# Layer 0's attention: the bias of two heads added as alternating 64-row tiles instead of one 128-row tile at a time

## What is computed

```python
B, N, C = x.shape                                   # 2, 1024, 128
H, D = (HEADS, C // HEADS)                          # 16 heads of 8
energy = jnp.einsum('bhqd,bhkd->bhqk', q, k)
pos = jnp.arange(N)
rel = pos[:, None] - pos[None, :] + (N - 1)
rel = jnp.clip(rel, 0, bias_table.shape[0] - 1)     # 0 .. 248
bias = bias_table[rel].transpose(2, 0, 1)
energy = energy + bias[None]
att = jax.nn.softmax(energy / (scaling * temp), axis=-1)
out = jnp.einsum('bhqk,bhkd->bhqd', att, v)
```

## Time and profile before

| | |
|---|---|
| timed executions | 1321.68, 1335.06, 1337.76 us |
| profiled execution, its own time | 1324.57 us |
| its span | 1322.7 us |
| TensorE busy | 1142.0 us, 86% |
| VectorE busy | 806.7 us, 61% |
| ScalarE busy | 650.9 us, 49% |
| layer 0's attention | about 228 to 663 us of the span |
| mean granted TensorE clock | 0.889 |

### The profile page before, as it was taken

How to read it: one execution, slowest core, us unless ns; L and a number is a source line. 1 busy time by engine, 2 the same in 40 slices (tenths; PEclk the granted TensorE clock), 3 DMA queues, 4 the chain that set the end, 5 groups by cost and what they waited for, 6 DMA issues and landing times.

```text
span 1322.7 us, 18522 instructions
## 1 busy us (share of the span) xinstructions
PE 1142.0 (86%) x6826; PEld 531.8 (40%) x6826; DVE 806.7 (61%) x1582; ACT 650.9 (49%) x1247; POOL 193.5 (15%) x309
## 2 busy tenths in 40 slices
PE   6599999999899999998884875899998889878577
PEld 4366666222222322232142432444443657434344
DVE  6633333878699889885056854787882524536554
ACT  4332222167477778777524143666777222414344
POOL 2146553001010011101000000112231000001000
PEclk9699999579799999999586586889999889899789
DMA  4521224133101101100006331110132300000321
GB/s 131 183 86 54 79 87 103 32 75 77 39 19 34 42 22 31 35 10 18 9 9 207 83 74 38 49 49 20 60 115 87 109 0 0 1 1 0 128 105 55
DMA packets 62165, 77.93 MB, mean 59 GB/s; under 512 B 15760, under 2 KB 39936, under 8 KB 60032
## 3 DMA queue, kind: packets, MB, share of 16 engines
q1 hardware_dynamic: 62080, 76.81, 19.1%
HBM read 61.58 MB, written 14.56 MB: 58 GB/s over the span
## 4 chain that ended last, share of the span: by engine, by line
PE 68%; DVE 13%; DMA 6%; SPq 5%; ACT 5%; issue 2%; POOL 0%; DVEq 0%; ACTq 0%
PE PS L1482 66%; DVE mx L1276 4%; ACT arena L877 3%; SPq L526 3%; DMA sums<-arena 2%; DMA arena<-k_dram 1%; SPq L533 1%; DVE arena L1455 1%; DVE small L1439 1%; SPq L544 1%; PE PS L1495 1%; DMA arena<-drev_dram 1%; DVE arena L1090 1%; DVE arena L1093 0%; DMA arena<-mrow 0%
## 5 line engine op out<-in xcount | busy, mean ns | idle before, releaser
L1482 PE MATMUL PS<-arena 128*32 128x512 f32 (+13 forms) x3656 | 626.9, 495 | 68.5 <-DVE mx L1276 39.3
L877 ACT ACTIVATE arena<-PS 128x512 f32<-128x512 f32 (+3 forms) x896 | 438.7, 556 | 271.3 <-PE PS L1482 267.5
L1276 DVE TENSOR_REDUCE mx<-PS 128x1 f32<-128x512 f32 (+3 forms) x896 | 506.5, 624 | 102.7 <-PE PS L1482 98.9
L1482 PEld LDWEIGHTS PS<-arena 128*32 128x32 f32 (+3 forms) x3656 | 160.2, 105 | 446.3 <-DVE mx L1276 181.2
L1482 PE MATMUL PS<-x_hi,w_hi_lo 128*128 128x512 f32 x320 | 145.1, 495 | 0.8 <-DVE combT L1154 0.4
L1377 DVE TENSOR_TENSOR fw<-PS,fw 128x512 f32<-128x512 f32 x80 | 55.3, 691 | 119.8 <-ACT fw L924 118.0
L924 ACT ACTIVATE fw<-PS 128x512 f32<-128x512 f32 x80 | 47.8, 597 | 123.5 <-PE PS L1482 123.5
L815 POOL TENSOR_TENSOR fw<-fw,arena 128x512 f32<-128x512 f32 x64 | 84.9, 1327 | 88.9 <-DVE fw L1377 88.9
L1482 PE MATMUL PS<-arena,fw 128*128 128x512 f32 x128 | 72.4, 680 | 24.7 <-DVE arena L1455 20.8
L1482 PE MATMUL PS<-fw 128*128 128x512 f32 (+3 forms) x184 | 90.6, 579 | 0.0
L768 POOL TENSOR_TENSOR arena<-arena,fw 128x512 f32<-128x512 f32 x32 | 41.7, 1304 | 268.7 <-DMA fw<-sum_dram 268.7
(11 more groups left out here) (268 smaller groups left out, 1035.4 us busy)
## 6 DMA issues: line engine op xcount, KB each, us to landing
arena<-comb_dram SPq DMA_DIRECT2D x16, 1024.0 KB, 5.1
fw<-sum_dram SPq DMA_DIRECT2D x32, 256.0 KB
arena<-comb_dram SPq DMA_DIRECT2D x16, 512.0 KB, 7.4
arena<-k_dram SPq DMA_DIRECT2D x16, 408.0 KB
q_dram<-arena SPq DMA_DIRECT2D x24, 256.0 KB, 3.8
k_dram<-arena SPq DMA_DIRECT2D x24, 256.0 KB, 3.9
arena<-q_dram SPq DMA_DIRECT2D x16, 384.0 KB
arena<-drev_dram SPq DMA_DIRECT2D x32, 192.0 KB, 3.7
```

Of the source, the lines that this page charges most:

```text
L877: s.activation(Pr[:, m % 8, 0:w], bank(4 + m % 3, 0, w), ACT.Exp).then_inc(A["e_done"], 1)
L1276: v.reduce_max(mx[:, H % 2, kh, n:n + 1], bank(U % RING, 0, w), axis=AX.X, negate=True).then_inc(A["ring_free"], 1)
L1482: return nc.tensor.matmul(out_, lhsT, rhs, start=start, stop=stop)
```

## The change

Per head and part, the bias now lies as two 64-row tiles in the row half in which that head's Q and K lie. `flip_sw` is `flip` with its row halves exchanged. Each former 128-row matmul becomes two 64-row ones, one for each half of the mirror. In ST these have 128 weight columns and 64 moving columns, half as many as before; in S five of six have 64 weight columns (half of the output's partitions) and the last one has 128, with 256 or 128 moving columns as before. The two heads of a pair (j even and j odd) are issued together: product, product, then the additions of both in turn. The tests `first_of_pair` and `second_of_pair` keep a pair in one slot of the plan. Layer 1 keeps its order.

```diff
@@ s_plan
+    if layer == 0:
+        marks = [n + first_of_pair(stream[n - 1]) for n in marks]
...
-            while i < len(steps) - 1 and done * t_total >= total * t_done:
+            while i < len(steps) - 1 and done * t_total >= total * t_done and not (layer == 0 and second_of_pair(what)):
@@ buffers
-        drev_dram = dram("drev_dram", (GROUPS, HG, PARTS, DREV), BF16)
+        drev_dram = dram("drev_dram", (GROUPS, HG, 2, PARTS, DREV), BF16)
+        flip_sw = sb("flip_sw", [P, P], BF16)
-        Hst = bf(132, 12).rearrange("p (s j a c) -> p s j a c", s=2, j=HG, a=PARTS)
+        Hst = bf(132, 12).rearrange("p (s r x c) -> p s r x c", s=2, r=PAIRS, x=2 * PARTS)
@@ load_bias
-                    src = bass.AP(tensor=drev_dram.tensor, offset=G * (HG * PARTS * DREV) + j * PARTS * DREV,
-                                  ap=[[1, P], [DREV, PARTS], [1, 256]])
-                    sp.dma_start(Hst[:, parity, j, :, :], src).then_inc(h_ld[parity], 16)
+                    row = 64 * (j % 2)
+                    src = bass.AP(tensor=drev_dram.tensor, offset=(G * HG + j) * 2 * PARTS * DREV,
+                                  ap=[[1, 64], [DREV, 2 * PARTS], [1, 256]])
+                    sp.dma_start(Hst[row:row + 64, parity, j // 2, :, :], src).then_inc(h_ld[parity], 16)
@@ stores of drev_dram, and the waits for them (16 * PARTS * BATCH * 2)
-                    dst = drev_dram[b * NG:(b + 1) * NG, :, part, :].rearrange("g j n -> (g j) n")
-                    sp.dma_start(dst, dpart[:, part, :]).then_inc(drev_stored, 16)
+                    for half in range(2):
+                        dst = drev_dram[b * NG:(b + 1) * NG, :, half, part, 0:DREV - 64 * half].rearrange("g j n -> (g j) n")
+                        sp.dma_start(dst, dpart[:, part, 64 * half:DREV]).then_inc(drev_stored, 16)
@@ GpSimd's constants: a memset of flip_sw and two affine_selects on it, ahead of const_done
+                    (flip_sw, [[1, P]], -(P // 2 - 1), 1, ALU.not_equal, 1.0),
+                    (flip_sw[:, :], [[1, P]], -(P + P // 2 - 1), 1, ALU.not_equal, 1.0),
@@ TensorE: additions to an S unit
-                        for part in range(PARTS):
-                            ins = mm(bank(U % RING, h0, 512), flip[:, :], Hst[:, G % 2, j, part, 0:512 - h0], start=False, stop=part == PARTS - 1)
+                        for part in range(PARTS):
+                            for half in range(2):
+                                rows = slice(64 - 64 * half, P - 64 * half) if (part, half) != (PARTS - 1, 1) else slice(0, P)
+                                pieces.append((dst[rows, h0:512], flip_of(row, half)[:, rows], Hst[row:row + 64, G % 2, pr, PARTS * half + part, 0:512 - h0]))
@@ TensorE: additions to an ST product
-                        extra = [(q * P, Hst[:, G % 2, j, part, P * (1 - q):P * (2 - q)]) for q in range(2) for part in range(PARTS)]
+                                for half in range(2):
+                                    cols = slice(64 - 64 * half, P - 64 * half)
+                                    pieces.append((dst[:, q * P + cols.start:q * P + cols.stop],
+                                                   Hst[row:row + 64, G % 2, pr, PARTS * half + part, x0:x0 + P], flip_of(row, half)[:, cols]))
@@ TensorE: the pair
+                def add_in_turn(adds, done):
+                    for n in range(len(adds[0])):
+                        for dst, weights, moving in (adds[0][n], adds[1][n]):
+                            ins = mm(dst, weights, moving, start=False, stop=n == len(adds[0]) - 1)
+                            if n == len(adds[0]) - 1:
+                                ins.then_inc(done, 1)
...
+                        elif first_of_pair(what):
...
+                            s_main(what, dst, False)
+                            if U + 1 >= RING:
+                                pe.wait_ge(A["ring_free"], U - RING + 2)
+                            s_main(other, dst2, False)
+                            add_in_turn((adds, s_adds(other, dst2)), A["ring_full"])
...
+                    elif j % 2 == 0:
+                        st_main(H, i, j, False)
+                        st_main(H, i, j + 1, False)
+                        add_in_turn((adds, st_adds(H, i, j + 1, bank(4 + (m + 1) % 3))), A["st_ps"])
```

More of the change, by code:

```diff
@@ L128, in s_stream, with first_of_pair, second_of_pair @@
     return stream + [(name, K) for name, K, k in late], ends
+def first_of_pair(what):
+    return what[0] == "S" and what[2] % 2 == 0
+def second_of_pair(what):
+    return what[0] == "S" and what[2] % 2 == 1
 def two_halves(layer, H):
@@ L712, in _ @@
             g.memset(sum_col[:, EXP:EXP + 1], 1.0)
-            for t_ in (ident, identb, flip, mask_kq, mask_qk, identb_sw, mask_kq_sw):
+            for t_ in (ident, identb, flip, flip_sw, mask_kq, mask_qk, identb_sw, mask_kq_sw):
                 g.memset(t_[:, :], 0.0)
@@ L1539, in attention, with flip_of, s_adds @@
                 A = att[l]
-                def mask(out_, row, weights, moving):
-                    for n, (w_, m_) in enumerate(zip(weights, moving)):
-                        ins = mm(out_, w_[row:row + 64, :], m_[row:row + 64, :], start=False, stop=n == 1)
-                    return ins
-                def s_unit(U, what):
+                def flip_of(row, half):
+                    return (flip, flip_sw)[(half + row // 64) % 2][row:row + 64, :]
+                def s_adds(what, dst):
@@ L1549, in s_unit @@
                     _, H, j, q, kh, w = what
                     G, pr, row = H // 2, j // 2, 64 * (j % 2)
-                    dst = bank(U % RING, 0, w)
-                    biased = l == 0 and q < 2 and kh == 1
-                    masked = l == 1 and q // 4 == kh
-                    ins = mm(dst, Qs[G][row:row + ROWS, pr, q * P:(q + 1) * P], Ks[G][row:row + ROWS, pr, 512 * kh:512 * kh + w],
-                             stop=not (biased or masked))
-                    if biased:
+                    if l == 0 and q < 2 and kh == 1:
@@ L1557, in s_unit @@
                         h0 = 256 if q == 0 else 384
+                        pieces = []
                         for part in range(PARTS):
-                            ins = mm(bank(U % RING, h0, 512), flip[:, :], Hst[:, G % 2, j, part, 0:512 - h0], start=False, stop=part == PARTS - 1)
-                    if masked:
-                        order = (identb, identb_sw) if row == 0 else (identb_sw, identb)
-                        masks = (mask_kq, mask_kq_sw) if row == 0 else (mask_kq_sw, mask_kq)
-                        ins = mask(bank(U % RING, w - P, w), row, masks, order)
```

79 lines of the change are left out of this document (55 added, 24 removed).

## The result

Over 20 executions each, the changed kernel takes 1321.48 us (median; 1312.55 to 1326.13) against 1329.93 (1317.5 to 1337.76): a ratio of 0.9946, 95% interval 0.9923 to 0.9969, or 7.2 us (4.1 to 10.2); the two medians themselves lie 8.45 us apart. The forecast had a gain nearly twice as large, 13.9 us. The forecast said 44.1.

What follows compares the result with a forecast made beforehand. TensorE was taken to bound the biased stretches, VectorE the plain ones. 7 x (0.5 + 1.2) + 0.5 + 1.5 = 13.9 us off a mean of 1329.8 gave about 1315 us (range 1300 to 1330), a group 44.1 instead of 45.83.

Steps and rivals of the forecast that it cites:

- What bounds the kernel: Layer 0 head groups: TensorE sets the pace in biased stretches, VectorE in plain ones; at most 3.84 us a group to win.
- Pitch: Spacing of 64-row ST additions within one row half: 0.042 us taken, between 0.027 (columns) and 0.056 (weight load).
- Row halves side by side: Additions of a pair's two row halves overlap, each half keeping its pitch; the rival without overlap gave 1355 us, chance 0.07.
- ST: Biased steps kt = 6 and 7: shorter additions, but second pairs wait for an exponential; gain 0.5 us a group (0.0 to 1.0).
- S: Biased S units in pairs with 64-row additions: gain 1.2 us a group, capped by VectorE's idle 2.06.
- Covered in the plain case: Late joint hand-over of S pairs is hidden: VectorE has up to 1.2 us of maxima left against about 1.1 of work.
- The first units: Group 0's eight biased S units ahead of the loop, at half clock: gain 1.5 us (1.0 to 2.0).
- `load_bias` keeps four DMAs of the same bytes: Bias loads cost nothing more with the new layout, as they run a group ahead.
- What costs nothing: Extra constants covered by TensorE's 3.32 us wait at 13.16; six more small stores and the bias loads also free.
- The sum: Seven groups' ST and S gains, one more ST gain and the first units: 13.9 us (6.6 to 24.4).
- VectorE's floor: Rival: biased stretches shrink until VectorE is the bound, gaining 30.6 us, time 1299 us; chance 0.15.
- The clock: Rival: half-microsecond waits drop TensorE to its lower clock level, eating the gain or costing 31 us; chance 0.08.

Runs made afterwards that it cites:

- s_single_full: Changed kernel with ST and S heads one at a time and all S additions with 128 weight columns: group 43.25 us.
- before_plan: Kernel before with only the new pair rule of the unit plan, heads single, 128-row additions: group 45.78 us, ratio 0.998.
- after_noS: Changed kernel with the S additions left out (S units single), ST in pairs with its 64-row additions: group 42.35 us.
- before_noS: Kernel before with the S additions left out, those to ST kept: group 43.13 us.
- st_single: Changed kernel with ST heads one at a time, S still in pairs: group 43.69 us.
- both_single: Changed kernel with its tiles and unit plan, but ST and S heads one at a time: group 44.79 us, ratio to before 0.9933.
- s_single: Changed kernel with S heads one at a time, ST still in pairs: group 45.79 us.
- after_noST: Changed kernel with the ST additions left out (ST products single), S in pairs with its 64x64 additions: group 42.95 us.
- before_noST: Kernel before with the ST additions left out, those to S kept: group 43.39 us.
- noadds_pairs: Changed kernel with all layer 0 bias additions left out, ST and S pairs kept: group 41.93 us.
- noadds_single: Kernel before with all layer 0 bias additions left out, order and loads as before: group 40.70 us.
- before_memset: Kernel before with only GpSimd's long memset moved behind VectorE's layer norm: group 45.83 us, TensorE's row at 13.16 comes 0.58 us sooner.
- best2: Changed kernel: single ST heads, full-width S pairs, later bias wait, flip_sw and memset moved, two S units per group moved into ST steps: group 43.58 us, ratio 0.9857.
- fixes: Changed kernel with single ST heads, flip_sw made after const_done, and group 0's four plain q = 1 units ahead of biased ones: group 43.70 us.

## Why the prediction was half right

**What bounds the kernel: right.** TensorE sets the pace in the biased stretches, VectorE in the plain ones (25.26 us whatever is done to the additions). The bound of 3.84 us a group was too small: without additions the group falls by 5.13.

**Pitch: too dear.** I took 0.042 us, from ends 0.027 and 0.056; it is 0.028, the low end. Columns set it, not the 128-column weights. The estimate of 53 ns from the Trainium skill ("TensorE: Matmul & The Clock Gate", LDWEIGHTS) does not hold here as a pitch.

**Row halves side by side: right**, in the earlier trace rows and here. But what the halves share is small beside what vanished: each head's change from 64-row products to 128-row additions and back: s_single_full, with no pair at all, has 43.25 us against before_plan's 45.78.

**ST: mechanism right, size low.** Forecast 0.5 us, measured 0.78. The waits for `e_done` came at the place given, before each step's second pair, 0.23 and 0.31 us; from A's last addition (426.75) to B's second product at 427.67 is 0.92, about 1.13 less 0.22. With the pitch of 0.028 the forecast's own sum gives 7.44 - 6.48 = 0.96. It left out the wait ahead of the first biased S unit: 0.43 us in after_noS against 0.22 at the same place in before_noS, and 0.96 - 0.21 = 0.75 is the measured 0.78 but for 0.03. What I didn't price either is the alternative: the pair was taken as given, and it costs 1.01.

**S: this step failed.** Forecast 1.2, measured 0.44. The work shrank as counted: from second product to the next ST product 0.88 us at q = 0 and 0.67 at q = 1, less 0.22 for the bare pair 0.66 and 0.45, against two heads' 1.06 and 0.76: 2 x (0.40 + 0.31) = 1.4 us a group. But TensorE now waits where it waited for nothing before: in and behind the pairs 0.13, 0.14 and 0.47 us, which st_single has too (0.14, 0.14, 0.47) and both_single and s_single, with S one at a time, have not. With ST's additions left out as well the account closes: after_noST waits 0.22 us ahead of the first pair, 0.14 twice inside pairs and 0.47 behind, 0.97 in all, before_noST at none of these places, and 1.42 - 0.97 = 0.45 against the measured 0.44. "Covered in the plain case" was wrong: the second product of a pair wants a second bank while VectorE is behind. "ScalarE is busy 7.64 of 11.30 us and takes that up" reads a share of busy time as slack: its idle time, 0.90 us, lies before the late product, and behind it the exponentials come in a row, so that the next ST product waits its 0.47:

```profile
443.40 1.57 ACT L892 ACTIVATE arena<-PS 128x512 f32<-128x512 f32 x3 [0.90 <-PE PS L1497]
```

**The first units: the work was right, the load failed.** 1.5 us forecast. The work gives more: from the end of the wait for the bias to the first M unit it is 16.77 us before (242.25 to 259.02) and 14.82 now (244.74 to 259.56), 1.95 less. The wait took it back, 2.09 us where it was 0.28, so that from the last up-projection product of the FFN to the first M unit it is 29.15 us before, 29.02 now. Faster units don't explain that wait: the same sixteen plain units stand ahead of it in both kernels, and noadds_pairs, without any additions, waits 1.95 us as well. `load_bias(0)` itself lands later. SyncE's queue, before and after:

```profile
222.04 13.89 SPq L533 DMA_DIRECT2D arena<-drev_dram  x4
```

```profile
223.27 15.04 SPq L545 DMA_DIRECT2D arena<-drev_dram  x4
```

The loads begin 1.23 us later, and from there to TensorE's start pass 21.5 us where it was 20.2; TensorE comes to the wait 0.68 later. noadds_single and noadds_pairs, whose loads begin at the same time (223.06 and 223.07), differ alike: TensorE starts at 243.24 and 244.12. So the step that failed is "`load_bias` keeps four DMAs of the same bytes", which put the new layout (64 partitions with six runs each, where it was 128 with three) at nothing; and for group 0 no load "runs a group ahead". Why this layout takes longer wasn't tried.

**"What costs nothing": failed for the constants.** The wait of 3.32 us at 13.16 was no cover (before_memset: it shrinks with VectorE's chain, to 2.73 us), since what TensorE waits for, VectorE's layer norm, was itself held by GpSimd's memset, and that moved with the constants: 0.65 us. The stores of `drev_dram` cost nothing visible, as said.

**The sum.** 7 x 1.13 + 0.7 for the last group's ST + 0.1 - 0.65 = 8.1 us, against the measured 7.2 (4.1 to 10.2). With the plan's 3 us at the start, which I hadn't foreseen, it is 11, 1 us above that interval. The profiled pair is further apart, and its M units show where. From the fifth on the changed kernel gains 1.1 us a group; ahead of that the large steps are two, 3.9 us from the first M unit to the second, and 3.4 from the fourth to the fifth. It is 14.1 us ahead at layer 0's last M unit (610.5 against 624.6) and loses 1.7 of it behind, where the code is unchanged. One reason that this can't be closed from single executions: behind the program's last M unit, in layer 1, the same code took 320.9 to 334.0 us in the 20 profiled ones. The base was right, 1329.8 against a median of 1329.93, and the change stayed within 2%, which had 0.73; the time lay inside the range.

**Rivals.** VectorE's floor wasn't reached, row halves do overlap. The clock stood at 1.00 from the fifth M unit on, in the changed kernel too, so half-microsecond waits didn't bring it down. Between the third M unit and the fifth it fell in both kernels, which is the place of the earlier trace rows. From the fourth M unit to the fifth, before and after:

```profile
337.09:366.70 29.61, 29.36 (x191) 8.72 (x190) 20.82 (x36) 18.07 (x34) 2.10 (x5) 0.84 0.15 38
```

```profile
333.15:359.35 26.20, 24.27 (x251) 7.37 (x250) 19.90 (x36) 17.39 (x33) 2.11 (x5) 0.92 0.17 42
```

The lower level came during a wait of TensorE of 6.42 us before and 5.92 now, and it reached less far into this stretch now. The 3.4 us lie here; over the 20 kernels the stretch took 22.1 to 29.6 us, and what sets the length of the lower level is open. The plan's 3 us at the start come with the clock's rise from 0.50 (1.2 GHz) to 1.00 (2.4 GHz) in the first stretch. Windows of before, then of before_plan:

```profile
278.00:282.00 4.00, 4.00 (x19) 0.81 (x23) 2.02 (x5) 2.37 (x6) 0.84 (x4) 0.52 0.20 60
```

```profile
274.00:278.00 4.00, 3.72 (x30) 0.78 (x22) 2.63 (x6) 2.56 (x6) 0.62 (x3) 0.95 0.20 70
```

The second kernel is at the upper level for nearly all of 274 to 278, the first still at the lower one from 278 to 281.8 (0.52). The same block took 23.3 to 24.9 us in the five kernels with the old plan and 20.9 to 21.9 in all with the new one (best2, with a third, 22.6); why the order of a few units brings the rise forward wasn't tried further.

## What to carry to other kernels

When freed work on one engine makes another wait in a new place, price the wait before the work: here 1.4 us of shorter additions in S brought 1.0 us of waits, and one product handed over at a time beat pairs in ST by 1.0 us a group. Keep neighbouring matmuls in one tile shape even at the price of computing zeros, and compare kernels by a period or by leaving a part out, not between boundaries that the edit itself moves. A wait that shows up at one place can come from an order somewhere else, so leave out one edit at a time before naming its owner. And price anew what an edit moves aside: the same bytes in another layout landed about 1 us later, and a constant "hidden" behind a wait delayed what that wait waits for.

## What the runs showed of the hardware

- A 64-row addition with 64 moving and 128 weight columns is issued every 0.028 us in one row half, with the other half busy or idle; with 256 moving columns every 0.107.
- A change between 64x128 and 64x64 tiles costs about 0.10 us each way, as the change between 128 and 64 rows did (0.32 against 0.22 on the way in, 0.20 against 0.11 on the way back).
- A small fp32 TENSOR_SCALAR on VectorE (0.18 us alone) took 1.40 us beside GpSimd's memset and ended with it (9.65 and 9.63); with the memset behind VectorE's work it took 0.17 to 0.18, in before_memset with no other edit. In `fixes` another TENSOR_SCALAR, begun at 9.16 under a memset of 8.29 to 10.10, took 0.97, while TENSOR_TENSORs under the same memset took 0.19. The Trainium skill ("SBUF — State Buffer", SBUF: two separate sides) describes a port pair that VectorE's faster modes and GpSimd lock for a whole instruction; the trace agrees.
